# A fused attention and feed-forward layer: the first feed-forward tiles cut by tokens around the last transpose, and three smaller moves

## The reference

```
q, k, v = x @ Wq.T + bq, x @ Wk.T + bk, x @ Wv.T + bv        # in heads
p = softmax(q @ k.T / sqrt(512)); p[nan] = 0; v[nan] = 0
p = p * triu                                                  # keeps keys at or behind the query
a = layernorm(x + p @ v) * gamma + beta
x = layernorm(x + a)                                          # "x2" in the kernel
h = silu(x @ W1.T * s1) * (x @ W2.T * s2)                     # layer 1, 1024 hidden features
h = gelu(h @ H1.T * s2h); h = gelu(h @ H2.T * s3h)            # layers 2 and 3
x = layernorm(x + h @ W3.T * s3)
```

## Time and profile before

| what | value |
|---|---|
| runs of the kernel | median 1259.55 us, 1258.51 to 1262.34 us |
| the profiled execution | 1263.22 us, its span 1261.1 us |
| PE busy in the span | 1180.7 us, 94% |
| DVE, ACT, POOL busy | 789.3, 528.9, 584.2 us |
| mean granted TensorE clock | 0.972 of full |

### The profile page before, as it was taken

How to read it: one execution, slowest core, us unless ns; L and a number is a source line. 1 busy time by engine, 2 the same in 40 slices (tenths; PEclk the granted TensorE clock), 3 DMA queues, 4 the chain that set the end, 5 groups by cost and what they waited for, 6 DMA issues and landing times.

```text
span 1261.1 us, 18179 instructions
## 1 busy us (share of the span) xinstructions
PE 1180.7 (94%) x7302; PEld 799.5 (63%) x7302; DVE 789.3 (63%) x1191; ACT 528.9 (42%) x698; POOL 584.2 (46%) x502
## 2 busy tenths in 40 slices
PE   4479999999999999999999999999999999999997
PEld 2134666747676576756667476765768466675786
DVE  3747676487656776476764776557764777647412
ACT  5777511564117621385115641176312751146311
POOL 5867522475226542375224742256422663246432
PEclk8569999999999999999999999999999999999999
DMA  9973631425334343246224263343532452332000
GB/s 335 275 184 72 186 80 39 119 66 170 68 86 102 134 101 69 52 102 197 59 48 115 57 183 68 86 102 115 120 69 52 103 173 61 69 69 70 1 1 17
DMA packets 55450, 128.47 MB, mean 102 GB/s; under 512 B 4032, under 2 KB 15680, under 8 KB 53312
## 3 DMA queue, kind: packets, MB, share of 16 engines
q1 hardware_dynamic: 51008, 115.44, 35.8%
q10 hardware_dynamic: 4352, 11.80, 2.8%
HBM read 88.95 MB, written 38.27 MB: 101 GB/s over the span
## 4 chain that ended last, share of the span: by engine, by line
PE 79%; DVE 7%; issue 4%; POOL 4%; DMA 3%; ACT 2%; ACTq 0%; POOLq 0%; DVEq 0%; SPq 0%
PE PS L981 50%; PE PS L898 9%; PE PS L917 6%; PE PS L866 6%; PE PS L828 3%; PE PS L924 3%; PE PS L930 2%; POOL diag_probs L437 2%; DVE neg_max L647 1%; DVE v_ones L637 1%; PE PS L845 1%; POOL raw_weights L505 1%; POOL rstd L450 1%; DMA raw_weights<-h1T_dram 1%; DVE x_tok L706 1%
## 5 line engine op out<-in xcount | busy, mean ns | idle before, releaser
L647 DVE TENSOR_REDUCE neg_max<-PS 128x2 f32<-128x1024 f32 x256 | 299.9, 1217 | 68.9 <-PE PS L866 68.9
L424 POOL TENSOR_TENSOR hidA_lo<-hidA_full,hidA_hi 128x512 fp32r<-128x512 f32 x128 | 167.8, 1311 | 259.7 <-DVE hidA_hi L796 194.4
L560 ACT ACTIVATE probsT<-PS 128x1024 f32<-128x1024 f32 x256 | 248.1, 1021 | 83.7 <-PE PS L898 83.7
L981 PE MATMUL PS<-hidA_hi,g 128*128 128x512 f32 x512 | 207.5, 405 | 0.0
L981 PE MATMUL PS<-hidC_hi,g 128*128 128x512 f32 x512 | 205.7, 402 | 0.0
L981 PE MATMUL PS<-hidA_lo,g 128*128 128x512 f32 x512 | 200.4, 391 | 0.0
L981 PE MATMUL PS<-hidC_lo,g 128*128 128x512 f32 x512 | 200.1, 391 | 0.0
L437 POOL TENSOR_TENSOR diag_probs<-probsT,mask 128x512 f32<-128x512 f32 x120 | 158.2, 1323 | 51.9 <-PE PS L981 31.1
L424 POOL TENSOR_TENSOR hidC_lo<-hidC_full,hidC_hi 128x512 fp32r<-128x512 f32 x64 | 82.5, 1290 | 213.0 <-DVE hidC_hi L796 213.0
L898 PE MATMUL PS<-stacks 66*128 66x512 f32 x512 | 153.2, 421 | 1.9 <-ACT probsT L560 1.9
L581 ACT ACTIVATE hidC_full<-PS,scales 128x512 f32<-128x512 f32 x64 | 44.1, 689 | 251.9 <-PE PS L981 251.9
(11 more groups left out here) (101 smaller groups left out, 1587.7 us busy)
## 6 DMA issues: line engine op xcount, KB each, us to landing
stacks<-qk_rows SPq DMA_DIRECT2D x64, 512.0 KB
stacks<-qk_rows SPq DMA_DIRECT2D x32, 1024.0 KB
qk_rows<-qk_hi SPq DMA_DIRECT2D x32, 512.0 KB, 3.7
qk_rows<-qk_lo SPq DMA_DIRECT2D x32, 512.0 KB, 5.7
xT_sb<-xT_dram SPq DMA_DIRECT2D x8, 512.0 KB, 4.2
raw_weights<-h1T_dram ACTq DMA_DIRECT2D x8, 512.0 KB, 10.2
raw_weights<-h2T_dram ACTq DMA_DIRECT2D x8, 512.0 KB, 7.9
x_tok<-x_dram SPq DMA_DIRECT2D x8, 512.0 KB, 6.2
```

The costliest lines, as they stand in the source:

```text
L424: nc.gpsimd.tensor_tensor(lo[:, m, :], full[:, m, :], hi[:, m, :], ALU.subtract).then_inc(lo_done, 1)
L560: nc.scalar.activation(PT[:, s % RING, 2 * pair:2 * pair + 2, :], PS[:, 2 * pair:2 * pair + 2, :], ACT.Exp, scale=SCALE).then_inc(exp_done, 1)
L647: nc.vector.tensor_reduce(NEGM[:, h // (H // 2), at:at + 2], PS[:, bank + 2 * side:bank + 2 * side + 2, :], AX.X, ALU.max, negate=True).th ...
L981: ins = nc.tensor.matmul(out, d if swapped else w, w if swapped else d, start=(k == 0 and part == 0), stop=(k == kts - 1 and part == 1))
```

## The change

Four edits. Behind part 0 of the turn, all four v tiles are projected at once, then tile m = 0 of layer 1 is done for the first 384 tokens (`first_layer(0, 0)`), then the last token tile is transposed (into bank 0 instead of 6), then m = 1 for 384 tokens, and then m = 0 and m = 1 for the last 128 tokens; `feed_forward` goes on with m = 2. The two halves of `guard_v` stand behind m = 2 and m = 5 of layer 1. POOL makes the low parts of q and k, all but the first, only when the last tile is normalized (it waits for `x2_ready`). The first addition of beta stands behind the masks of step 6, not of step 5.

```diff
-X_AT = (5, 8, 12, 13)
+X_AT = (6, 8, 12, 13)
+        GUARD_AT = {2: 0, 5: 1}
...
-            return PS[:, 6, 0:DT * P].rearrange("p (c s) -> p c s", c=DT), slice(X2_CUT, S)
+            return PS[:, 0, 0:DT * P].rearrange("p (c s) -> p c s", c=DT), slice(X2_CUT, S)
...
                 rstd(b, QT - 1, 0)
-                if not last:
-                    split_qk(b + 1, range(1, 2))
                 rstd(b, QT - 1, 1)
                 if not last:
-                    split_qk(b + 1, range(2, 2 * DT))
+                    after(pool, x2_ready, b, QT, QT)
+                    split_qk(b + 1, range(1, 2 * DT))
...
-            def guard_v(b):
+            def guard_v(b, part):
+                if part == 0:
+                    after(dve, v_taken, b, 1, 1)
+                    after(dve, out_stored, b, 16, -16)
+                    nc.vector.tensor_scalar(negative, v, 0.0, None, ALU.min).then_inc(v_step, 1)
+                else:
+                    after(dve, v_step, b, 1, 1)
+                    nc.vector.scalar_tensor_tensor(out=v, in0=v, scalar=0.0, in1=negative,
+                                                   op0=ALU.max, op1=ALU.add).then_inc(v_ready, 1)
...
-                if not last:
-                    guard_v(b + 1)
+                    if not last and m in GUARD_AT:
+                        guard_v(b + 1, GUARD_AT[m])
...
-                    after(pe, qk_biased, b, 2 * DT, 2 * DT + 1)
+                    after(pe, qk_biased, b, 2 * DT, 2 * DT + 3)
...
-                for m in range(HT):
+                for m in range(0 if general else 2, HT):
...
+            def first_layer(b, last, m, part):
+                after(pe, x2_split, b, 2, part + 1)
+                if m == 0 and part == 0 and not last:
+                    after(pe, qk_biased, b, 2 * DT, 2 * DT + 2)
+                tokens = (slice(0, X2_CUT), slice(X2_CUT, S))[part]
+                for which, w in ((0, W1), (1, W2)):
+                    for k in range(DT):
+                        for d in (X2hi, X2lo):
+                            ins = nc.tensor.matmul(PS[:, bank1(m, which), tokens], w[:, k, m * P:(m + 1) * P],
+                                                   d[:, k, tokens], start=(k == 0 and d is X2hi),
+                                                   stop=(k == DT - 1 and d is X2lo), skip_group_check=True)
+                    if part == 1:
+                        ins.then_inc(ffn1, 1)
...
                 turn_x2(b, 0, last)
                 if not last:
                     project(b + 1, range(DT, 2 * DT))
-                    project_v(b + 1, range(2))
+                    project_v(b + 1, range(QT))
                 else:
-                    keep_warm(7, 18)
+                    keep_warm(7, 20)
+                if not general:
+                    first_layer(b, last, 0, 0)
                 turn_x2(b, 1, last)
-                if not last:
-                    project_v(b + 1, range(2, QT))
-                else:
-                    keep_warm(7, 2)
+                if not general:
+                    first_layer(b, last, 1, 0)
+                    first_layer(b, last, 0, 1)
+                    first_layer(b, last, 1, 1)
```

More of the change, by code:

```diff
@@ L628, in v_rows @@
                 return VXT[:, 0:QT * VX].rearrange("p (r e) -> p r e", e=VW)[:, :, 0:HD]
-            def guard_v(b):
-                after(dve, v_taken, b, 1, 1)
-                after(dve, out_stored, b, 16, -16)
+            def guard_v(b, part):
                 v, negative = v_rows(), Vm[:].rearrange("p t (h e) -> p (t h) e", e=HD)
[L635 to L638, removed]
+                if part == 0:
[6 more added lines that the diff above has]
+                                                   op0=ALU.max, op1=ALU.add).then_inc(v_ready, 1)
             def row_max(b, unit, bank=0):
@@ L803, in _ @@
             take_v(0)
-            guard_v(0)
+            guard_v(0, 0)
+            guard_v(0, 1)
             sum_squares(0)
@@ L1056, in attention, with next_projections @@
                     project_half(b + 1, 1, 1)
-            def next_projections(b, last):
+            def first_layer(b, last, m, part):
[11 more added lines that the diff above has]
+                        ins.then_inc(ffn1, 1)
+            def next_projections(b, last, general):
                 if last:
@@ L1077, in body @@
                         attention(b)
-                    next_projections(b, last)
+                    next_projections(b, last, general)
                     feed_forward(b, last, general)
```

## The result

In five rounds on one chip the changed kernel took **1251.27 us** in the median (1248.73 to 1253.6), the kernel before 1257.19 to 1264.0. The ratio is **0.9912**, with a 95% interval of 0.9885 to 0.9940, so some 11 us less (7.6 to 14.5); the two medians alone, 1259.55 and 1251.27, are 8.3 apart. Forecast were 1250 us and a gain of 9.5.

A forecast was written before the change was run, and what follows sets the result against it. PE was taken as the bound, working 94% of the 1261.1 us span. Terms 9.0 + 0 - 0.7 + 1.2 = 9.5 us turn the 1259.55 median into 1250; own range 1246 to 1254.5, 8-in-10 range 1246 to 1259.

The forecast's parts named there:

- Last tile's instructions without their neighbour: At the turn, DVE's two normalizing instructions drop from 1.39 and 1.35 us to 0.49 and 0.41 without POOL beside them.
- Narrow products: Layer 1's sixteen 128-column products for the last tokens take 0.12 us each, 1.92 in all.
- The rival of 0.22: Layer 1's 128-column rounded products run no faster than plain f32, 0.22 us each, 3.5 for sixteen; chance 0.12.
- the slower case: Whole kernel 2.4 us slower, 1262 us, if the 128-column products take 0.22 us each; chance 0.12.
- m = 2: Third tile of layer 1 on PE begins at 438.60 instead of 439.03, a gain of 0.4 us.
- The chain on the lock: In layer 1, DVE and POOL alternate on the shared port: low parts 1.66 us apart, v's second repair pushing POOL by 0.87.
- POOL first: POOL gets the port first at m = 5; the repair costs 2.0 us instead of 0.87, total 1258 us; chance 0.08.
- k = 7: In layer 2, the products needing layer 1's last low part begin at about 453.7 instead of 454.00, gain 0.3 us.
- A boundary: Passage between batches, up to the second unit of next-batch scores: 1.5 us gained at each of six, 9.0 in all.
- Boundary 0: First passage between batches: m = 2 starts later, but that loss eats the 0.92 us wait for maxima; gain 0.
- The last batch: No q, k or v there, so the first products wait for the low part: a loss of 0.7 us.
- X_AT: In attention, moving the beta addition behind step 6's masks frees POOL earlier: 0.17 us in each of seven batches, 1.2 total.

The follow-up runs named there:

- no_parts: Changed kernel without the layer-1 token parts (POOL split, v repair inside layer 1 and X_AT edit on the kernel before); ratio 0.9868 to the kernel before.
- pool_guard: Kernel before with POOL's q and k split moved and the v repair inside layer 1, old X_AT, no token parts; ratio 0.9881.
- x_only: Kernel before with only the X_AT edit, the first addition of beta behind the masks of step 6; ratio 0.9958.
- parts_only: Kernel before with only layer 1's tiles m = 0 and 1 done in two token parts around the last transposes; ratio 1.0039.
- pool_back: Changed kernel with POOL's pieces of q and k put back ahead of the last normalized tile; ratio 0.9969 to the kernel before.
- x_tile_first: Changed kernel without the token parts, x loaded in two transfers, token tile 0 first; median 1235.39 us, ratio 0.9796 to the kernel before.
- all_and_x_tile: Changed kernel, token parts included, with x loaded in two transfers, token tile 0 first; ratio 0.9870 to the kernel before.

## Why the prediction was right

Its steps, one by one, at the boundary of batch 2 (places are counted from the first six transposes):
- **Last tile's instructions without their neighbour**: forecast 0.49 and 0.41, measured 0.48 and 0.42. The three pieces behind it take 3.75 (forecast 3 x 1.29), and nothing waits for their store, as costed.
- **Narrow products**: forecast 0.12 each and "not under" 0.107; measured (431.60 - 431.38)/2 = 0.11, over more of them 0.111. That is near the 0.107 of their weight loads, which fits the reason given; no run shows it apart. Sixteen take 1.8 us, 0.7 more than the 1.06 at 0.066. The Trainium skill, "TensorE: Matmul & The Clock Gate", "LDWEIGHTS (loading the stationary operand)", has columns / 1.2 for such a load, 107 ns for 128; from it the prediction estimated sixteen at 0.9 us more than by columns alone, and the trace agrees in size. The rival of 0.22 is out, and with it the slower case. Products of 384 columns take 0.173 to 0.175, forecast 0.174.
- **m = 2**: forecast 0.4 earlier, measured 0.64 (12.31 against 12.95); the gate is 0.8 later, forecast 0.9.
- **The chain on the lock**: forecast 1.66 a tile, and it is 1.66. L639 gets the port first, takes 1.21 (forecast 1.09) and pushes POOL by 0.92 (forecast 0.87). So the rival "POOL first" did not come about: in the seven kernels with the repair inside, this instruction took 1.21 to 1.22 at each of the seven boundaries. k = 7, the eighth pair of low and high parts in layer 2, begins 0.46 earlier (27.43 against 27.89), forecast 0.3.
- **A boundary**: forecast 1.5, measured 1.44. Two misses nearly cancel here: k = 7 comes 0.16 earlier than forecast, and from it to the second unit are 1.59 us, forecast 1.36. **Boundary 0**: forecast 0; its second unit stands 30.72 us behind the transposes, where it was 30.65, with the same 5.3 us for the products of k in both. (Its own working, 1.1 lost at m = 2 and the wait of 0.92 won, gives -0.2 and not 0; m = 2 came 0.9 later.) **The last batch**: forecast -0.7; m = 2 stands 11.15 us behind its transposes, where it was 10.58, so -0.6.
- **X_AT**: forecast 0.17 a batch, 1.2 in the sum. The periods show 0.24 to 0.48 (no_parts against pool_guard, x_only and changed against before). At an equal landing of x it is 0.14 to 0.24, so 1.0 to 1.7 us; the rest is the landing. The size was thus about right. Missing was a term for the load itself, whose landing moves the period by as much as it scatters.

The sum with the measured terms is 6 x 1.44 - 0.6 + 1.0 to 1.7 = 9.0 to 9.7, against the 9.5 of the forecast, the 8.3 between the medians and the 11 of the ratio. (The two ends of the prediction's range are a little off its own terms: with the others as they stand, 2.1 a boundary gives 13.1, not 13.5, and a chain 0.8 later 1254.9, not 1254.5.)

What the prediction had in its numbers and did not draw from them is that the parts are a loss. It said that "the PE time won at the turn is thus mostly not seen as such: it is spent on narrow products and on the chain", and went on to price the edits as one. The split on POOL by itself already has the last tile ready 1.8 us earlier, more than the 1.31 that PE waited for it. What the parts add is 16 x (0.173 + 0.111) = 4.54 us of products in place of 16 x 0.228 = 3.65: 0.9 us of PE, on the engine that bounds the kernel. The first unit of scores stands at 25.18 in the changed kernel and at 24.23 in no_parts, 0.95 apart, which is this term. At the second unit they are 1.18 apart: a tenth is the wait for the last low part (k = 7 begins 0.33 behind the product before it, where products follow at 0.23). The last tenth is the first product behind that wait: the next one follows it at 0.34 (448.17 to 448.51), where in no_parts it is 0.23. Over six boundaries the parts gave back some 7 us of the 16 that the two other edits had won.

Left open: single ratios hang together with the periods only to about 0.3%. x_only shows 5 us (2.6 to 7.9) where its period says 3.3, parts_only 5 us slower (1.6 to 8.2) where its boundaries and last batch add up to some 2, pool_back as said above. The scatter of the start (127.5 to 134.0 us for the first turn) is as large as these. The sign of parts_only rests on its ratio and on the boundary; the loss by the parts beside the other edits rests on two pairs of kernels.

## What to carry to other kernels

When an edit bundle removes two waits, look for the smallest edit that removes each: here one moved instruction group on a neighbour engine did for the turn what a new product order was also built for. Filling a wait of the bounding engine with work that must be cut narrow for it is no gain when the wait can be removed: the cut's price is paid every time. When the waits of one stage are gone, read the next stage's at once; the late transfer in attention was worth another 0.56 us a batch for one split load. And before a small difference of two profiles is called an edit's, compare the time of each load that the stage waits for: a quarter of a us here looked like a gain and was an earlier landing.

## What the runs showed of the hardware

- Products in the rounded type with 128 columns follow each other at 0.111 us, with 384 at 0.173 and with 512 at 0.228: the line through the last two gives 0.118 at 256 columns, which is what such products take, but 0.063 at 128. So 128 columns run above that line, and if 0.111 is a floor, little is saved below some 240 columns (an estimate from where the line passes 0.111; no product between 128 and 256 columns was run).
- L639 on DVE ran for 1.21 us, and POOL's instruction that started 0.15 us after it became 0.92 longer: 2.20 to 2.22 in place of 1.29 at all seven boundaries of the seven kernels with the repair inside.
- The time from issue to landing of one 512 KB load scattered between 5.0 and 6.8 us from batch to batch, and with the old `X_AT` the part of the period outside the boundary followed it by 0.99 us for each us over 30 batches. With x in two transfers that part stayed at 116.2 to 116.5 us in twelve batches of x_tile_first and all_and_x_tile, while the first transfer took 6.0 to 7.5 us. The first turn of the program stood between 127.5 and 134.0 us from kernel to kernel.
